# GpSimd's token norms and output gating behind the third norm, two scan steps earlier, the gates in two pieces

## The reference, cut to what matters

```python
# layer 0
xn = layernorm(x)
s  = latent attention of xn, 16 heads of 8, causal            # scores, exp, weighted sum of values
logits = cos(xn, centroids) + xn @ w_route.T                  # cos needs 1/|xn| of each token: "token norms"
gates  = softmax over the two largest of 8 logits
x = x + s * silu(sum_e gates[e] * (gelu(xn @ w1[e] + b1[e]) @ w2[e] + b2[e]))
# layer 1
xn2 = layernorm(x)                                            # the kernel's second norm
h   = layernorm(xn2) * gamma + beta                           # its third norm
k, v, q = h @ Wk.T + bk, h @ Wv.T + bv, h @ Wq.T + bq
for t in tokens:  y[t] = W q[t];  W = W - 0.01 * (W k[t] - v[t]) k[t].T     # linear recurrence
x = x + (xn2 + y) * silu(xn2 @ sign(weight).T)                # its output gating
```

## Time and profile before

| what | value |
|---|---|
| median of 3 runs | 709.38 us (709.02 to 711.78) |
| profiled execution | 706.64 us, of which the span from the first to the last instruction is 704.2 us |
| mean granted TensorE clock | 0.953 |
| busy: PE, DVE, ACT, POOL | 603.2, 419.5, 363.6, 171.6 us |

### The profile page before, as it was taken

How to read it: one execution, slowest core, us unless ns; L and a number is a source line. 1 busy time by engine, 2 the same in 40 slices (tenths; PEclk the granted TensorE clock), 3 DMA queues, 4 the chain that set the end, 5 groups by cost and what they waited for, 6 DMA issues and landing times.

```text
span 704.2 us, 16715 instructions
## 1 busy us (share of the span) xinstructions
PE 603.2 (86%) x6886; PEld 389.3 (55%) x6886; DVE 419.5 (60%) x1033; ACT 363.6 (52%) x742; POOL 171.6 (24%) x322
## 2 busy tenths in 40 slices
PE   4487898999897999898998989798998998896864
PEld 2143464566564755566564756575565665553653
DVE  1366666666758476857667575947676665414341
ACT  3200646845664556645674465645673667473310
POOL 4373103222314111412223121511231202212111
PEclk9999999999998999999998999899999999998675
DMA  2663001610142004310251014300330000000000
GB/s 75 154 174 86 1 8 32 156 40 2 54 115 66 8 10 114 86 36 2 76 128 33 7 31 105 99 8 10 103 94 23 2 9 16 23 1 3 1 17 15
DMA packets 28870, 35.59 MB, mean 51 GB/s; under 512 B 3932, under 2 KB 25243, under 8 KB 27643
## 3 DMA queue, kind: packets, MB, share of 16 engines
q1 hardware_dynamic: 28794, 34.53, 19.2%
HBM read 24.46 MB, written 9.96 MB: 49 GB/s over the span
## 4 chain that ended last, share of the span: by engine, by line
PE 58%; DVE 18%; issue 8%; ACT 7%; POOL 6%; DMA 1%; SPq 1%; POOLq 0%; DVEq 0%; ACTq 0%
PE ps_v L843 8%; PE ps_s L824 8%; PE ps_e L809 6%; DVE cand L1313 4%; PE ps_a L771 4%; PE ps_a L759 4%; PE ps_e L806 3%; PE ps_s L827 3%; DVE second L1258 3%; PE ps_a L734 2%; PE ps_c L908 2%; DVE stats L1244 2%; DVE hid L1297 1%; PE ps_c L982 1%; PE ps_c L890 1%
## 5 line engine op out<-in xcount | busy, mean ns | idle before, releaser
L1313 DVE TENSOR_REDUCE cand<-ps_s 128x4 f32<-128x512 f32 (+1 forms) x320 | 213.0, 684 | 75.3 <-PE ps_s L827 54.6
L1118 ACT ACTIVATE prob<-ps_e 128x512 f32<-128x512 f32 x320 | 187.8, 596 | 106.5 <-PE ps_e L809 102.6
L824 PE MATMUL ps_s<-kst,qst 72*128 72x128 bf16 (+1 forms) x1024 | 132.8, 246 | 23.1 <-DVE cand L1313 22.5
L809 PE MATMUL ps_e<-qst,kst 75*128 75x384 bf16 (+3 forms) x512 | 124.0, 304 | 0.0
L824 PEld LDWEIGHTS ps_s<-kst,qst 72*128 72x128 bf16 x1024 | 76.1, 103 | 84.6 <-DVE cand L1313 55.3
L843 PE MATMUL ps_v<-prob,vaug 128*32 128x512 f32 (+3 forms) x1024 | 91.8, 456 | 0.0
L806 PE MATMUL ps_e<-identb,negmask 128*128 128x256 bf16 (+1 forms) x320 | 81.8, 256 | 10.9 <-ACT prob L1118 10.8
L809 PEld LDWEIGHTS ps_e<-qst,kst 75*128 75x128 bf16 x512 | 50.9, 99 | 18.6 <-issue 1.2
L827 PE MATMUL ps_s<-negmask,identb 128*128 128x512 bf16 x128 | 52.9, 413 | 0.0
L615 POOL CAST mparts<-nm 128x32 bf16<-128x32 f32 x16 | 3.4, 210 | 172.7 <-DVE nm L1320 172.7
L806 PEld LDWEIGHTS ps_e<-identb,negmask 128*128 128x128 bf16 x320 | 31.7, 99 | 22.2 <-ACT prob L1118 18.3
(11 more groups left out here) (315 smaller groups left out, 950.4 us busy)
## 6 DMA issues: line engine op xcount, KB each, us to landing
qst<-q_scratch SPq DMA_DIRECT2D x48, 192.0 KB
kst<-k_scratch SPq DMA_DIRECT2D x16, 576.0 KB
q_scratch<-qparts SPq DMA_DIRECT2D x24, 128.0 KB, 2.3
k_scratch<-kparts SPq DMA_DIRECT2D x24, 128.0 KB, 2.2
xn<-in_L_attn_x_dram SPq DMA_DIRECT2D x8, 256.0 KB, 3.1
x_res<-in_L_attn_x_dram SPq DMA_DIRECT2D x8, 256.0 KB, 2.9
out_dram<-second SPq DMA_DIRECT2D x7, 256.0 KB, 2.4
max_scratch<-mrow SPq DMA_DIRECT2D x16, 96.0 KB, 1.7
```

Source lines behind the costliest of these rows:

```text
L809: last = mm(ps_e[:, bank, at:at + TOK - P * j], k[0:SROWS, hd, tok(j)], q[0:SROWS, hd, P * j:TOK], start=False, stop=True, skip_group_chec ...
L824: last = mm(ps_s[:, bank, w * n:w * (n + 1)], q[0:PAIRS, hd, tok(i)], k[0:PAIRS, hd, keys[0]:keys[1]], start=(n == 0), stop=True, skip_gro ...
L1118: af(prob[:, u, :], ps_e[:, u % 2, :], ACT.Exp).then_inc(S["e_emptied"], 1)
L1313: vec.tensor_reduce(cand[:, i, h0:h0 + FILLS * (len(hds) - 1) + 1:FILLS, S_SLOT[u]], ps_s[:, u % 2, :].rearrange("p (a c) -> p a c", a=len ...
```

## The change

1. `rn` and `c_out` go behind `ln3_norm` in the table, and on POOL both get a wait on the third norm of `prev` (four increments of `norm2`, one for each scaled block).
2. `c_y2` and `c_r3`, which stood after the first two units of the next iteration, go into step 4 of the iteration before, `c_y2` behind PE's last weighted sums and before `v`, and `c_r3` behind `yt`. `c_u3` and `c_y3` move up by two units and one.
3. `gates` ends after `dlt` and `keep`; the rest of its DVE part and its whole POOL part are a new piece `gate_norm` one unit later, behind `lev_a1`.
4. POOL's part of the first norm (`ln1_rstd`) goes ahead of `m_parts0`.
5. The numbers that the waits count to are no longer constants: one walk over the same schedule counts, for each bank, how many pieces fill it before a given one. Where the order is unchanged they are the same, with one exception: the third norm's wait for the tile that it overwrites counts to `lev_d6` of the sequence before and no longer to its `c_y3`.

```diff
 PLAN = {
-    (0, 0): ["c_y2"], (0, 1): ["c_r3", "gb0"], (0, 2): ["ln2_stats", "c_u3"], (0, 3): ["c_y3"], (0, 4): ["gb1", "ln2_norm"],
-    (0, 5): ["rn"],
-    (0, 6): ["pv0", "c_xn2t", "ln3_stats", "c_out", "gb2"], (0, 7): ["ln3_norm"], (0, 8): ["gb3"], (0, 9): ["pv1", "c_ht"],
+    (0, 0): ["c_u3"], (0, 1): ["gb0"], (0, 2): ["ln2_stats", "c_y3"], (0, 4): ["gb1", "ln2_norm"],
+    (0, 6): ["pv0", "c_xn2t", "ln3_stats", "gb2"], (0, 7): ["ln3_norm", "rn", "c_out"], (0, 8): ["gb3"], (0, 9): ["pv1", "c_ht"],
     (1, 0): ["load_x", "c_kt", "c_qt", "m_rows1"], (1, 1): ["c_vk", "out"], (1, 2): ["c_gram", "pv2"], (1, 3): ["logits"],
-    (1, 4): ["yt", "c_ffn", "gates"], (1, 5): ["lev_a1"], (1, 6): ["pv0"], (1, 7): ["lev_d1"], (1, 8): ["gt"],
-    (1, 9): ["pv1", "lev_a2"], (2, 0): ["ln1_stats", "lev_d2", "m_parts0"], (2, 2): ["ln1_rstd", "ln1_norm", "lev_a3", "pv2"], ...
+    (1, 4): ["yt", "c_ffn", "gates"], (1, 5): ["lev_a1", "gate_norm"], (1, 6): ["pv0"], (1, 7): ["lev_d1"], (1, 8): ["gt"],
+    (1, 9): ["pv1", "lev_a2"], (2, 0): ["ln1_stats", "lev_d2", "ln1_rstd", "m_parts0"], (2, 2): ["ln1_norm", "lev_a3", "pv2"], ...
...
-    (3, 9): ["pv1", "c_u2"], (4, 0): ["m_parts1", "gelu", "stacks1"], (4, 1): ["pv2"], (4, 2): ["v"], (4, 3): ["yt", "x1"],
+    (3, 9): ["pv1", "c_u2"], (4, 0): ["m_parts1", "gelu", "stacks1"], (4, 1): ["pv2", "c_y2"], (4, 2): ["v"], (4, 3): ["yt", "x1", "c_r3"],
...
 LAST_PLAN = {
-    (0, 0): ["last:zero_state", "c_y2"], (0, 1): ["c_r3"], (0, 2): ["gb0", "ln2_stats", "c_u3"], (0, 3): ["c_y3"], (0, 4): ["gb1"],
-    (0, 5): ["ln2_norm", "c_out"], ...
+    (0, 0): ["last:zero_state", "c_u3"], (0, 2): ["gb0", "ln2_stats", "c_y3"], (0, 4): ["gb1"],
+    (0, 5): ["ln2_norm"], ... (1, 4): ["yt", "ln3_norm", "c_out"], ...
...
             def token_norms(b):
...
                 pool.wait_ge(S["ssm_ready"], b.count(1, 1))
+                after(pool, S["norm2"], NT * (b.c - 1))
                 after(pool, S["cos_ready"], b.count(1, 0))
...
             def c_out(b):
                 r, o = second_layer(b)
-                pool.wait_ge(r.S["c1_emptied"], o.count(C1_FILLS, C1_Y + 1))
+                pool.wait_ge(r.S["c1_emptied"], C1_NUMBER[b.c, "c_y3"] + 1)
+                if b.c < SEQS - 2:
+                    pool.wait_ge(S["norm2"], NT * (b.c + 2))
...
             def ln_norm(n, b):
...
                 elif n == 2:
-                    after(dve, r.S["c1_filled"], o.count(C1_FILLS, 0))
+                    if o.c > 0:
+                        dve.wait_ge(r.S["c1_filled"], C1_NUMBER[b.c - 1, "lev_d6"] + 1)
```

More of the change, by code:

```diff
@@ L114 @@
 }
-HEAD = ("load_x", "ln1_stats", "ln1_rstd", "ln1_norm", "xnt", "q", "k")
+HEAD = [(name, 0) for name in ("ln1_stats", "ln1_rstd", "ln1_norm", "xnt", "q", "k", "rn_first")] + [
+    ("prepare", None), ("load_x", 1), ("stacks0", 0), ("stacks1", 0)] + [
+    (name, 1) for name in ("ln1_stats", "ln1_rstd", "ln1_norm", "xnt", "q", "k", "stacks0", "stacks1")] + [("masks", None)]
 PLAN_SECOND = ("load_x", "ln1_stats", "ln1_rstd", "ln1_norm", "xnt", "q", "k", "stacks0", "stacks1")
-PLAN_NEXT = ("rn", "logits", "gates", "gt", "h0", "h1", "h2", "h3", "gelu", "v", "m_parts0", "m_rows0", "m_parts1")
-PLAN_OLDER = ("c_y2", "c_r3", "c_u3", "c_y3", "c_out")
+PLAN_NEXT = ("rn", "logits", "gates", "gate_norm", "gt", "h0", "h1", "h2", "h3", "gelu", "v", "m_parts0", "m_rows0", "m_parts1")
+PLAN_OLDER = ("c_u3", "c_y3", "c_out")
 PLAN_CURRENT = ("gb0", "gb1", "gb2", "gb3", "out", "pv0", "pv1", "pv2", "yt", "x1", "m_rows1", "zero_state")
@@ L159, in head_of, with iteration, schedule, numbers @@
     return FH * (grp // FILLS) + FILLS * hh + grp % FILLS
[L162 to L167, removed]
-    if b.c == 0 and n < 0:
-        return n - A_XNT
-    if b.c == SEQUENCES - 1 and n >= A_H:
-        return n - 3
-    return n
+def iteration(second, nxt, cur, prev, older, plan=PLAN):
+    for step in range(1 + max(at[0] for at in plan)):
+        for u in range(UNITS):
+            if step < GROUPS:
+                yield "unit", (cur, nxt, step, u)
+            for name in plan.get((step, u), []):
+                of = second if name in PLAN_SECOND else nxt if name in PLAN_NEXT else \
+                    cur if name in PLAN_CURRENT or name.startswith("last:") else older if name in PLAN_OLDER else prev
+                name = name.removeprefix("last:").removeprefix("prev:")
+                if of is not None:
+                    yield name, (of, step) if name in ("pv0", "pv1") else (of, step - 1) if name in ("pv2", "yt") else (of,)
+def schedule():
+    seqs = [Seq(c) for c in range(SEQUENCES)]
+    for name, c in HEAD:
+        yield name, () if c is None else (seqs[c],)
+    yield from iteration(None, seqs[0], None, None, None)
+    yield "settle", ()
+    for t in range(2, SEQUENCES):
+        yield from iteration(*(seqs[t - behind] if t >= behind else None for behind in range(5)))
+    yield from iteration(None, *seqs[:SEQUENCES - 5:-1])
+    yield from iteration(None, None, *seqs[:SEQUENCES - 4:-1], plan=LAST_PLAN)
+def numbers(pieces, last_apart=False):
+    table, count = {}, [0, 0]
+    for piece, at in schedule():
+        if piece in pieces:
+            own = int(last_apart and at[0].c == SEQUENCES - 1)
+            table[at[0].c, piece] = count[own]
+            count[own] += 1
+    return table
+A_NUMBER = numbers(A_PIECES)
+C0_NUMBER, C1_NUMBER = numbers(C0_PIECES, True), numbers(C1_PIECES, True)
 def after(eng, sem, value):
@@ L885, in c_vk @@
                 r, o = second_layer(b)
[L886 removed]
+                for bank, fill, filled, n in ((r.ps_c0, c0_fill, "c0_filled", "c_vk"), (r.ps_c1, c1_fill, "c1_filled", "c_vk")):
                     fill(b, n)
@@ L988, in c_y @@
                 if c == 0:
-                    c1_fill(b, C1_Y)
-                pe.wait_ge(r.S["c0_emptied"], o.count(C0_FILLS, c0_u(c) + 1))
+                    c1_fill(b, "c_y3")
+                pe.wait_ge(r.S["c0_emptied"], C0_NUMBER[b.c, f"c_u{c}"] + 1)
                 if c > 0:
@@ L1011, in _ @@
                 pieces[f"c_y{c}"] = lambda b, c=c: c_y(b, c)
-            run(pe, pieces, unit, prepare, settle)
+            run(pieces | {"unit": unit, "prepare": prepare, "settle": settle})
         @block.scalar
@@ L1190, in _ @@
             pieces[f"lev_d{IN_SQUARE}"] = lev_d
-            run(act, pieces, unit, prepare)
+            run(pieces | {"unit": unit, "prepare": prepare})
         @block.vector
@@ L1433, in _ @@
                 pieces[f"lev_a{lv}"] = lambda b, lv=lv: lev_a(b, lv)
-            run(dve, pieces, unit, prepare, settle)
+            run(pieces | {"unit": unit, "prepare": prepare, "settle": settle})
 PREP_OUT = 18
```

224 lines of the change are left out of this document (89 added, 135 removed), and 6 rows, old and new, of tables (LAST_PLAN, PLAN).

## The result

| | median | runs | profiled execution | span | mean granted clock |
|---|---|---|---|---|---|
| before | 709.20 us (707.09 to 711.78) | 4 | 706.64 us | 704.2 us | 0.953 |
| changed | 683.75 us (682.55 to 688.74) | 4 | 682.94 us | 680.6 us | 0.961 |

The ratio is 0.9654, with the 95% interval 0.9604 to 0.9704: 25.4 us less, where 21.9 were forecast (687.5 against the 709.38 known then).

The account below looks back on a forecast made before the run. PE, busy 86%, was taken to bound the kernel, waiting on DVE scalings held by POOL. Terms -11.1 + 1.0 - 5.2 + 0 - 5.7 = -21.0 gave 685.6 from 706.64 or 688.4 from the median; chosen 687.5 us, range 682 to 698.

Parts of the forecast that it names:

- Gating and norms behind the third norm: Second norm: its scaling falls from 3.15 to 1.11 us once POOL's gating is moved; 11.1 us less in all.
- Scan steps: Iteration's end: three multiplications delay the residual and so the second norm; +0.2 us per iteration, +1.0 in all.
- First norm: Its power comes sooner; of PE's 1.06 us wait, 0.2 is lost to small POOL instructions; -5.2 us in all.
- Gates: Gates in two pieces: PE's 0.74 us wait goes, but the transposed gates come later; taken as 0.
- The clock: Three clock falls behind the second norm's stall, 1.9 us each, taken as gone with it; -5.7 us.
- the clock falls anyway: Rival, whole kernel: the falls stay although the stall goes, so 5.7 us isn't had; 694 us, chance 0.2.
- The collision at the first norm: Rival: small POOL instructions hold the first norm's scaling, so its 5.2 us gain shrinks to 1.0; 691.7 us, chance 0.14.
- the wait without effect: Rival: the second norm keeps its 3.15 us and the clock falls stay; 705.2 us, chance 0.07.
- The rival of the late scan step: Rival: ACT's u_sb copy comes behind gelu, delaying values, transposes and residual 3.2 us per iteration; near 713 us, chance 0.03.

Follow-up runs that it names:

- e7: The changed kernel plus one extra POOL instruction, of another kind or size each iteration, beside the second norm; 689.23 us, one execution timed.
- e5: The changed kernel without its first part (token norms and output gating again ahead of the third norm); 690.76 us, undisturbed iteration 73.98 us.
- e2: The kernel before with only the first norm's POOL power moved ahead of the splitting of the maxima; 699.94 us, ratio 0.9874.
- e1: The kernel before with only the token norms and output gating put behind the third norm; 696.73 us, undisturbed iteration 74.30 us.
- e3: The kernel before with only the scan steps moved (c_y2, c_r3, and the two behind them earlier); 699.52 us, undisturbed iteration 75.46 us.
- e4: The kernel before with only the gates in two pieces; 708.73 us, ratio 0.9981 (0.9951 to 1.0011), undisturbed iteration 75.97 us.
- e6: The changed kernel with scan steps c_y2 and c_r3 back at the start of the next iteration; 683.09 us, undisturbed iteration 72.70 us.
- e8: The changed kernel with DVE's two block copies after lev_d4 replaced by subtractions that read PSUM; 688.15 us, 73.15 us an iteration.
- e9: The changed kernel with DVE's two block copies after lev_d4 one unit later; 683.26 us, 72.52 us an iteration.
- e12: e10 with the block copies one reduction further on, just ahead of krest; 680.2 us, 72.20 us an iteration.
- e10: e9 with scan steps c_y2 and c_r3 also back at the start of the next iteration; 681.85 us, 72.20 us an iteration.

## Why the prediction was right, and where its terms were off

The forecast of 687.5 us lies 3.8 above the median, inside its own range of 683 to 692. The undisturbed iteration came out at -3.17, where the terms gave -2.04 + 0.2 - 0.86 = -2.70. That the sum is this near is partly luck: without the clock the terms gave 15.3 us and the profiled spans about 19.2 (23.6 less 4.4), 3.9 more, and the clock term was 1.3 too large. By its steps:

**Gating and norms behind the third norm (-2.04 per iteration).** Right in mechanism and size: the stretch from the second norm to the third, 7.01 us before, is 4.98. In e7 a block was held until POOL's instruction ended. The Trainium skill's rule ("SBUF — State Buffer", Who interferes with whom), that the two engines exclude each other for whole instructions, agrees with that for the products and the copy. It doesn't agree with the power of 1.05 us, which held no block, nor with the memset, behind whose held block the next one came through almost at once; here the measurements decide. The prediction said that small POOL instructions had so far not run beside a scaling; this power of 128x4 had, in every full iteration of the kernel before (370.59 above is one). Alone this part gave 1.90. But its value isn't its own: with the scan steps moved it is 0.95 (e5).

**Scan steps (+0.2, bounds -0.5 to +0.7 per iteration).** +0.33 in the changed kernel, by the way that was forecast: the residual starts 0.67 us later behind the table load, and the second norm 0.34 later (9.88 us behind it, 9.54 before). The working considered only PE's additions and the residual; it didn't ask what it does to the collision that the second norm starts earlier. In the whole change that question is moot; by itself the edit gains 0.74.

**First norm (-0.86, and "the most that can be had" 1.06).** Both too small; the gain is 1.23. The cap was read from the idle time in the earlier trace rows, and that is short of the loss: PE's group at 332.71 has a modelled duration of 0.39, while the next started 1.45 us after it. In the changed kernel the same two starts, at 323.70 and 323.92 above, lie 0.22 apart, and 1.45 - 0.22 = 1.23. The 0.2 that I took off for the collision was for nothing. Alone (e2) it is 1.2 as well.

**Gates (0).** -0.23 per iteration; the sum of the four is then -2.04 + 0.33 - 1.23 - 0.23 = -3.17, the whole difference. It comes out with 2.04 and not with the 1.90 of e1, since the 0.12 us that e1 lost again ahead of the first norm isn't lost once that norm's power comes first.

**The clock (-5.7).** The step that failed: "Where it goes, I take them as gone." The stall went and falls stayed. In the profile of before three full iterations have one, at 1.84 to 1.88 us; in the changed kernel one full and the first iteration do. The one at 440 us begins with PE at work in full:

```profile
438.00:440.00 2.00, 1.28 (x12) 0.69 (x16) 1.70 (x5) 0.34 (x2) 1.46 (x3) 1.00 0.00 0
440.00:442.00 2.00, 2.00 (x19) 0.96 (x12) 2.00 (x5) 0.47 (x1) 1.40 (x2) 0.50 0.00 0
442.00:444.00 2.00, 2.00 (x11) 1.35 (x10) 0.78 (x2) 0.98 (x2) 1.92 (x2) 0.65 0.00 0
444.00:446.00 2.00, 2.00 (x13) 1.05 (x12) 0.17 (x1) 1.54 (x3) 0.22 (x1) 1.00 0.39 111
```

It lasts some 3 us, against 6 before, and costs 1.16 instead of some 1.86. What brings it on isn't shown: the last long wait of PE ahead of it is 0.93 us for `hid`, which ends at 438.51, but the iteration before has the same one and no fall:

```profile
365.48 0.39 PE L733 MATMUL ps_a<-gT,pick 96*128 96x512 bf16 x1 [0.92 <-DVE hid L1270]
```

Over the full iterations falls gave 4.4 us. The rival "the clock falls anyway" (694) was thus half right in what it says, and its time was wrong because the other terms were larger than I had them.

The collision at the first norm fell with its scaling at 1.11 us and its longest block of 376 ns, and the wait without effect with the second norm's at 1.11. The rival of the late scan step fell with the residual, which POOL starts 3.38 us after the table load and not 2.71: 0.7 us later, where the rival had 3.9. The time of that rival was also added up wrongly: its own numbers give 709.4 - 22.0 + 6 x 3.9 = 710.8, not 713.

The gains of the four parts alone, by the medians, add to 31.4 us against 25.4 for the whole. In the iteration they add to 4.1 (1.90, 1.23, 0.74, 0.23) against 3.17, and what lies between them is for the most part the held block that e1 and e3 both remove, 1.09 us.

## What to carry to other kernels

- A stall by collision depends on when two lists meet, so any edit ahead of it on either engine moves it by whole instructions. Ask of each edit what it does to the meeting time, and don't add gains that were measured alone.
- Read the price of a wait on PE from one start to the next and compare it with the same pair unhindered; the idle time shown is short by the pipelined part of the last instruction.
- When single effects are below the scatter of whole runs, cut the trace at an instruction that comes once per iteration and compare iterations with the same granted clock.

## What the runs showed of the hardware

- A 128x128 block of a scaling from SBUF to SBUF on DVE (0.34 us) is held by a product or a copy of 128x128 to 128x512 on POOL, whatever the tiles are: it ended 0.08 us behind POOL's instruction, after 0.42 to 1.06 us in e7 and up to 1.42 us before. POOL's multiplication took 1.38 to 1.42 us beside the scaling and 1.27 us without it.
- A memset of 0.66 us held one block and cost the four 0.10 us; a copy of 0.66 us cost them 0.29. A power of 128x4 that lasted 1.04 to 1.09 us held none. A subtraction that reads PSUM wasn't held by a cast (0.58 us for the pair).
- The clock's falls don't follow the length of the stall simply. With PE's wait of 2.03 us, three, two and four of four full iterations had one (before, e4, e2); with 0.94 us, none in e3 and e5; with no wait at that place, one or two in e1, e6, e8, e9, e12 and both executions of the changed kernel, and none in e10. What decides between these stays open.
